# Score operand stacks of 112 rows, loaded by wide transfers, in a decoder layer with an alignment stage

## What is computed

```
x = x + attention(layernorm(x))        # causal, 16 heads of 16 features
x = x + align(context, layernorm(x))   # dynamic time warping, 77 x 1024 distances per batch
x = x + ffn(layernorm(x))              # 256 -> 1024, butterfly, gelu, butterfly, -> 256
```

```
q = (h @ Wq) / 4;  k = h @ Wk;  v = h @ Wv
A = (q @ k.T) ** 2, masked to the causal part
o = (A @ v) / (A.sum(-1) + 1e-5);  out = o @ Wo
```

## Time and profile before

| | us |
|---|---|
| median of 3 runs | 951.19 |
| lowest and highest | 950.64, 962.34 |
| profiled execution, its own time | 949.06 |
| its span in the profile | 947.3 |
| PE busy | 784.5 (83%) |
| DVE busy | 555.7 (59%) |
| ACT busy | 437.5 (46%) |

### The profile page before, as it was taken

One profiled execution on the slowest core, in us unless ns is written; L12 is line 12 of the kernel. 1 busy time (PEld: TensorE's weight loads), 2 busy tenths in 40 slices (PEclk: granted clock), 3 DMA queues, 4 the chain that ended last, 5 costly groups with the idle time before them and its releaser, 6 DMA issues.

```text
span 947.3 us, 12610 instructions
## 1 busy us (share of the span) xinstructions
PE 784.5 (83%) x3919; PEld 379.3 (40%) x3919; DVE 555.7 (59%) x2527; ACT 437.5 (46%) x664; POOL 143.1 (15%) x310
## 2 busy tenths in 40 slices
PE   3879998999998987867979969869699642699998
PEld 2444332543321632122343212434484532457657
DVE  3833275334724350899999998469789888521000
ACT  1127869667688566554747657233204100133120
POOL 2202313312211212202112211110001000100100
PEclk9879999999997999779989889989899967599999
DMA  9890585525366506061850662010010001100001
GB/s 297 195 146 1 67 167 94 95 25 67 136 85 61 66 2 81 15 77 38 174 70 9 77 75 40 14 23 9 6 48 12 12 23 45 30 1 12 33 1 45
DMA packets 52178, 58.58 MB, mean 62 GB/s; under 512 B 22675, under 2 KB 31863, under 8 KB 52111
## 3 DMA queue, kind: packets, MB, share of 16 engines
q1 hardware_dynamic: 51023, 53.57, 32.8%
q0 software_dynamic: 1088, 4.19, 1.3%
HBM read 36.24 MB, written 21.50 MB: 61 GB/s over the span
## 4 chain that ended last, share of the span: by engine, by line
PE 43%; DVE 36%; ACT 8%; issue 7%; DMA 4%; SPq 1%; DVEq 0%; POOL 0%; ACTq 0%; POOLq 0%
PE psO L1042 7%; PE psS L1025 7%; PE psW L1181 7%; PE psS L1171 6%; DVE FOLD L807 6%; DVE FOLD L828 6%; ACT ARENA L666 4%; PE psW L1080 4%; DVE FOLD L805 3%; DVE FOLD L826 3%; DVE FOLD L804 3%; PE psW L1087 2%; PE psW L1100 2%; DMA MORE<-dist 2%; DVE FOLD L825 2%
## 5 line engine op out<-in xcount | busy, mean ns | idle before, releaser
L666 ACT ACTIVATE ARENA<-psS 128x1024 f32<-128x1024 f32 (+3 forms) x384 | 295.2, 811 | 96.3 <-PE psS L1025 92.8
L1025 PE MATMUL psS<-ARENA 96*128 96x512 bf16 (+3 forms) x768 | 189.3, 341 | 24.5 <-ACT ARENA L666 22.7
L1042 PE MATMUL psO<-ARENA 128*32 128x512 f32 (+3 forms) x1536 | 170.7, 517 | 14.8 <-DVE ARENA L762 12.9
L604 POOL TENSOR_SCALAR_AFFINE_SELECT ARENA<-ARENA 128x256 f32<-128x256 f32 x256 | 109.3, 432 | 426.8 <-ACT ARENA L666 423.7
L1025 PEld LDWEIGHTS psS<-ARENA 96*128 96x128 bf16 x768 | 53.8, 99 | 209.8 <-ACT ARENA L666 143.3
L1181 PE MATMUL psW<-W2E,ARENA 128*128 128x256 f32 x512 | 114.2, 384 | 22.0 <-DVE ARENA L1005 21.3
L1181 PEld LDWEIGHTS psW<-W2E,ARENA 128*128 128x128 f32 x512 | 98.1, 192 | 38.4 <-DVE ARENA L1005 22.1
L729 ACT ACTIVATE ARENA<-psS,BEFF 128x512 f32<-128x512 f32 x64 | 43.6, 687 | 122.8 <-PE psS L1171 122.8
L1080 PE MATMUL psW<-XX,ARENA 128*128 128x512 f32 x128 | 66.0, 650 | 9.5 <-DVE ARENA L909 5.2
L807 DVE TENSOR_TENSOR_SCAN FOLD<-FOLD,MORE 64x37 f32<-64x37 f32 x208 | 65.2, 314 | 7.3
L1071 PE MATMUL psW<-IDENT,XX 128*128 128x128 f32 x192 | 33.0, 319 | 43.4 <-DVE XX L895 43.0
(11 more groups left out here) (116 smaller groups left out, 826.0 us busy)
## 6 DMA issues: line engine op xcount, KB each, us to landing
ARENA<-qk_parts SPq DMA_DIRECT2D x192, 128.0 KB, 7.2
qk_parts<-ARENA SPq DMA_DIRECT2D x16, 768.0 KB, 4.5
out<-ARENA SPq DMA_DIRECT2D x16, 256.0 KB, 2.2
X<-in_x POOLq DMA_DIRECT2D x3, 1024.0 KB, 9.2
dist<-ARENA SPq DMA_DIRECT2D x4, 425.0 KB, 10.5
MORE<-dist SPq DMA_DIRECT2D x32, 52.6 KB
path<-MORE SPq DMA_DIRECT2D x52, 32.4 KB
dist<-ARENA SPq DMA_DIRECT2D x4, 300.5 KB
```

Source lines behind the costliest of these rows:

```text
L604: pool.affine_select(out=blk, in_=blk, compare_op=ALU.is_ge, fill=0.0, base=0, pattern=[[0, 2], [1, P]], channel_multiplier=-1).then_inc(s ...
L666: nc.scalar.activation(A[:, (2 * G + a) % A_PAIRS, :, 0:N], psS[:, a, :, 0:N], ACT.Square).then_inc(s_sq, 1)
L1025: ins = nc.tensor.matmul(psS[:, a, j, 0:N], KST[0:STACK, g % 2, 2 * a + j, kt * P:(kt + 1) * P], QST[0:STACK, g % 2, 2 * a + j, q0:q0 + N] ...
L1042: ins = nc.tensor.matmul(psO[32 * j:32 * j + 32, o % 2, q0 - qc * HALF:q0 - qc * HALF + N], V1[:, kt, GH * g + j], A[:, (2 * G + j // 2) % ...
```

## The change

The tensor in HBM is ordered by head: for each of q and k, for each head, its three parts of 16 rows stand one after another. A part of 16 rows of 1024 tokens, and also the three parts of a head, are then one contiguous block. The stack has 112 rows in place of 96: rows 0 to 47 hold q parts 0, 1, 2, rows 48 to 95 the same once more, rows 96 to 111 q part 0. Against them stand k part 0 three times, k part 1 three times, and k part 2. One product of parts is added (q part 2 with k part 1); the others are those of before, in another order.

A stack is loaded by 14 transfers in place of 12. For each of the four heads there is one for `QST` over 96 partitions, whose source is the 48 rows of the head repeated twice, and two for `KST` over 48 partitions, whose source is 16 rows repeated three times; and there are two over 16 partitions for the last block of all four heads. A stack is 1792 KB in place of 1536 KB. `parts_out` issues three transfers, one for each part, where it issued one. The waits on the two semaphores change with the number of transfers.

```diff
-Q_PART = [0, 0, 0, 1, 1, 2]
-K_PART = [0, 1, 2, 0, 1, 0]
-STACK = len(Q_PART) * HD
+WIDE = 2 * PARTS * HD
+STACK = WIDE + HD
+STACK_DMAS = 3 * GH + 2
+PART_DMAS = 2 * PARTS
...
-    qk_dram = nc.dram_tensor("qk_parts", (B, 2, PARTS, D, L), BF16, kind="Internal").ap()
+    qk_dram = nc.dram_tensor("qk_parts", (B, 2, NH, PARTS, HD, L), BF16, kind="Internal").ap()
...
             def parts_out(b, m):
                 for i in range(2):
                     sp.wait_ge(s_split, b * 8 + 4 * m + 2 * i + 2)
-                    dst = qk_dram[b, i].rearrange("c (m p) t -> m p c t", m=2)[m]
-                    sp.dma_start(dst, QP[:, m, i]).then_inc(s_parts_out, 16)
-                sp.wait_ge(s_parts_out, b * 64 + 32 * (m + 1))
+                    heads = qk_dram[b, i, m * NH // 2:(m + 1) * NH // 2]
+                    for c in range(PARTS):
+                        sp.dma_start(heads[:, c], QP[:, m, i, c]).then_inc(s_parts_out, 16)
+                sp.wait_ge(s_parts_out, 16 * PART_DMAS * (2 * b + m + 1))

             def stack_in(b, g):
                 if b * NG + g >= 2:
                     sp.wait_ge(s_qk, (b * NG + g - 1) * 2 * NS // NG)
-                for slot in range(len(Q_PART)):
-                    rows = slice(slot * HD, (slot + 1) * HD)
-                    for i, (dst, part) in enumerate(((QST, Q_PART), (KST, K_PART))):
-                        src = qk_dram[b, i, part[slot]].rearrange("(g j d) t -> g d j t", g=NG, j=GH)[g]
-                        sp.dma_start(dst[rows, g % 2], src).then_inc(s_stack[g % 2], 16)
+                for j in range(GH):
+                    h = GH * g + j
+                    sp.dma_start(QST[0:WIDE, g % 2, j], qk_dram[b, 0, h].rearrange("c d t -> (c d) t").unsqueeze(0).to_broadcast(
+                        [2, PARTS * HD, L])).then_inc(s_stack[g % 2], 16)
+                    for x in range(2):
+                        sp.dma_start(KST[x * PARTS * HD:(x + 1) * PARTS * HD, g % 2, j], qk_dram[b, 1, h, x].unsqueeze(0).to_broadcast(
+                            [PARTS, HD, L])).then_inc(s_stack[g % 2], 16)
+                for i, (dst, part) in enumerate(((QST, 0), (KST, PARTS - 1))):
+                    sp.dma_start(dst[WIDE:STACK, g % 2], qk_dram[b, i, GH * g:GH * (g + 1), part].rearrange("j d t -> d j t")
+                                 ).then_inc(s_stack[g % 2], 16)
...
-                    pe.wait_ge(s_stack[g % 2], 16 * 2 * len(Q_PART) * (2 * b + g // 2 + 1))
+                    pe.wait_ge(s_stack[g % 2], 16 * STACK_DMAS * (2 * b + g // 2 + 1))
```

More of the change, by code:

```diff
@@ L652, in _ @@
                     if i == 0 and b:
-                        act.wait_ge(s_parts_out, 64 * b)
+                        act.wait_ge(s_parts_out, 32 * PART_DMAS * b)
                     if i == 0 and b == 3:
@@ L677, in _ @@
                     if i == 0 and b + 1 < B:
-                        act.wait_ge(s_parts_out, 64 * max(b + 2, 3))
+                        act.wait_ge(s_parts_out, 32 * PART_DMAS * max(b + 2, 3))
                     act.wait_ge(s_ready, ready(*u))
@@ L901, in _ @@
                     if i == 0 and b:
-                        dve.wait_ge(s_parts_out, 64 * b)
+                        dve.wait_ge(s_parts_out, 32 * PART_DMAS * b)
                     if i == 0 and b == 3:
```

## The result

The changed kernel takes 1090.12 us, the median of four runs, against 952.17 of the kernel before in the same sessions: a ratio of 1.142, interval 1.134 to 1.150. It is 138 us slower. 1041 was forecast, in a range of 985 to 1100. The profiled execution has a span of 1088.7 us, 141.4 over the 947.3 of before.

What follows compares the result with a forecast made beforehand. The prediction took stack loads as covered before, but slowed to two engines by the change, 504 of 528 us on the fullest. Stalls totalling 92 us on 949.06 gave 1041 us, range 985 to 1100.

Steps and rivals of the forecast that it cites:

- The rule: All transfers: engines used must divide the outermost count of both sides, so Q loads get 2, K loads 3, parts 8.
- Rival (a): Stack loads: all 16 engines serve every load, a stack takes 6.2 us, total 942 us; chance 0.11.
- the terms: 112 rows on PE taken as 0; parts out 8.0 us for each m in place of 4.0.
- 27.5 us a stack: Stack load: the fullest engine carries 672 kB at 24.4 GB/s, 27.5 us in place of 13.1.
- the 2 us added for its landing: End of each stack load: 2 us added until the data has landed.
- the two tails over 16 rows: Last block of a stack: two transfers put 8 + 8 KB on the fullest engine.
- 504 of 528 us: Fullest engine: 16 stacks at 27.5 and 8 parts at 8.0 us, within the window from 38.5 to 567.
- by nothing: Stack 0, first load: lands at 68.5 us, just in time for its group at 68.7.
- late, forecast: Walk through the stack queue: group starts slip against the kernel before, summing to 91.9 us by group 15.
- eight stalls of the forecast: Groups 2, 4, 7, first distances, groups 11, 12, 14, 15: 14.5, 12.5, 10.8, 14.0, 3.2, 14.5, 14.3, 8.1 us.
- (b): Stalls on PE: lateness mostly absorbed by DVE and ACT catching up, only 14.5 + 12.5 us count, 976 us; chance 0.05.
- (c): Stack loads: one engine alone 30% slower, 36 us a stack, 1080 to 1110 us; lower PE clock 15 more; chance 0.06.

Runs made afterwards that it cites:

- rows_even: Changed kernel's rows and bytes, memory laid out head, feature, part, token so outermost dimensions are multiples of 16 on both sides: 949.93 us, 0.998 of the kernel before.
- parts alone: Kernel before with memory by head and parts out in three transfers each on 8 engines, stacks still 96 rows: 956.49 us, ratio 1.004.
- k_sixteens: Changed kernel with each K load over 48 partitions split into three loads of 16, Q's repeat kept: 991.75 us, 1.042 of the kernel before.
- q_halves: Changed kernel with each Q load over 96 partitions split into two of 48, K's repeat kept: 967.45 us, 1.015 of the kernel before.
- q_repeat_only: rows_even with Q's repeat of 2 outermost again and the eight K loads ahead of the Q loads: 1001.65 us, 1.054 of the kernel before.

## Why the prediction was right, and by how much not

**The rule.** That a transfer runs on as many engines as divide the outermost count of both sides was the step on which all hung. Before, only transfers whose two sides agree had shown it. It holds for differing sides too: 51,151 packets, 2.1 engines by share, 24.5 GB/s each. This agrees with the divisor rule of the Trainium skill (DMA: Bandwidth & Descriptors, "Why a DMA increments its semaphore by 16 and not by 1"). Rival (a) fell, and rows_even shows what (a) would have been: 950, not the 942 that I gave it, since a stack took 9 to 10 us and not 6.2.

**PE and parts.** 112 rows cost nothing on PE (340 against 341 ns), and parts alone 5 us, inside the terms.

**The size.** 92 us were forecast, 141 came in the span. The mis-sized term is "27.5 us a stack" and the 2 us added for its landing. Stack 3 is issued back to back between 132.9 and 162.7, 29.8 us; a stack that starts on an idle queue takes 32.7 from first issue to first matmul (111.5 to 144.2), not 29.5, and the others for which PE waited take 32.2 to 32.8, stack 4 left out. The engines' rate fits the forecast: 24.5 GB/s each against 24.4. There is a start, of which I had counted only the end: nothing moves from 111.5 to 112.5, and 8 GB/s in the microsecond behind. And the two tails over 16 rows, priced by bytes at 0.7 us, cost more than their bytes. SP issues those of stack 2 from 131.0 to 132.8. Fourteen engines with little left to do run their share of them in one burst, while the two full engines still have Q and K loads before them, as the rate and the order of issue suggest:

```profile
133.00:134.00 1.00, 0.00 (x0) 0.00 (x0) 0.00 (x0) 0.00 (x0) 0.00 (x0) 0.50 0.73 180
134.00:135.00 1.00, 0.00 (x0) 0.00 (x0) 0.00 (x0) 0.00 (x0) 0.00 (x0) 0.50 0.36 53
135.00:136.00 1.00, 0.00 (x0) 0.00 (x0) 0.00 (x0) 0.00 (x0) 0.00 (x0) 0.50 0.17 41
136.00:137.00 1.00, 0.00 (x0) 0.00 (x0) 0.00 (x0) 0.00 (x0) 0.00 (x0) 0.50 0.14 53
```

Between 132 and 137 the queue moves 86 GB/s, 430 kB. Less the fourteen engines' 229 kB of the tails, 201 are left, where two full engines alone would move 245: about 1 us lost, an estimate. The rest of the 2.3 us by which 29.8 exceeds 27.5 was not placed.

Three us a load are no small thing where the sum of all loads was already 504 of 528 us. Stack 0, in time "by nothing", is 5.6 late: the parts ahead of it land at 41.8 and not at 38.5, and the load takes 32.6. Group 1 is 2.8 more, without a wait for its stack. And at groups 2, 4 and 7, the first distances, and groups 12 and 14 the stalls are 16.0, 20.1, 20.1, 18.4 (49.04 less the 30.68 of before), 20.6 and 19.9 us, where 14.5, 12.5, 10.8, 14.0, 14.5 and 14.3 were forecast:

| start of group | 0 | 1 | 2 | 4 | 7 | 10 | 12 | 14 | 15 |
|---|---|---|---|---|---|---|---|---|---|
| late, forecast | 0 | 0.3 | 14.5 | 27.0 | 37.8 | 51.8 | 69.5 | 83.8 | 91.9 |
| late, measured | 5.6 | 8.4 | 24.5 | 46.6 | 67.8 | 87.5 | 114.1 | 133.8 | 137.2 |

Stacks 4 and 7 missed most, by 8 and 9 us: before each, two stacks and the parts of a batch follow one another on the same engines, and each adds its excess; on stack 4 lies also the load of the last weights, and it takes 35.5 us. Of the eight stalls of the forecast seven are there, each longer than forecast. The eighth isn't: at group 11, 3.2 us forecast, PE does not wait for the stack; it waited 7.6 us there for DVE, and the lateness grew by 9.7. Behind the last group 2.6 us are added where nothing was to change.

**Rivals (b) and (c).** Most of (b) falls: between the starts of two groups lateness never fell by over 2 us. But not every stall counted in full: the last three, 20.6, 19.9 and 10.7 us, added 16.8, 16.7 and 3.4, because the groups ahead of them ran shorter than in the kernel before. Of (c), one engine alone was not slower than its sixteenth part, but the other half was there: behind the stalls PE came back at the lower of its two clock levels, 0.50 in the windows 143 to 147, 228 to 230, 348 to 351 and 670 to 671. The forecast had put this at nothing. The groups behind the stalls at 0, 2, 4, 7 and 12 grew by another 2.8, 1.9, 2.6, 1.4 and 3.1 us; these 12 us together are the most that the clock can have cost there, and its own share was not measured apart.

## What to carry to other kernels

Before a transfer is made wider, look at the outermost dimension of both sides as the code writes them. Here a side that begins with a repeat of 2 or a loop over 8 heads put the whole transfer on 2 or 8 engines, and the cure was another order of dimensions, not fewer rows. The packet count of the queue, less the runs that the code names, tells how many engines the transfers used. When a hidden load becomes faster, little is won; when it becomes slower, all that goes beyond its cover is lost. Put the transfer that has a waiter ahead of the one that has a cover.

## What the runs showed of the hardware

- Closing packets are one for each engine that a transfer used: all counts above (51,023, 51,151, 53,071, 48,975, 48,591) come out exactly, and so do the packets of 4 bytes by themselves, such as 9,203 in k_sixteens.
- Issuing is held when the engines that a transfer needs are full: a K load's issue took 0.68 us at least and 5.66 at most, against 1.11 at most for the same K loads in q_halves, and SP stood at L447 for 14% of the chain, with all later transfers behind it, those for idle engines too.
- Two engines busy all the time move 49 GB/s, and show in the profile as a DMA share of only 0.13; a low share is no sign of an idle queue.
- With all engines busy, loads into rows 0 to 47 moved some 150 GB/s and those into rows 48 to 95 some 260 (rows_even, 40 to 42 and 44 to 46), loads over 16 rows 120, parts out over 128 rows 382 and X coming in 400.
- One issue in 0.63 us is a limit of its own: eight even loads of 96 KB in a row moved 142 to 154 GB/s with the engines less than half busy (q_repeat_only).
